# A routing stage and an expert stage joined into one block, with semaphore waits where the engines used to meet

## The chip, the cores and the metric

The kernel runs on one core of one Trainium2 chip. The metric is the time of one execution on the device in microseconds (us). The kernel before took 1334.64 us, the median of three runs (1334.37 to 1336.47).

The engines are named as the profile names them: PE is TensorE (matrix products), DVE is VectorE, ACT is ScalarE, POOL is GpSimd, SP is SyncE (here it only issues DMAs). A q behind a name is that engine's instruction sequencer.

## The reference

The reference is a network on a graph of 3125 nodes with 256 features and 50000 edges: a graph convolution, an attention over slices, a second graph convolution, and a mixture of experts. The change touches the last of the four alone:

```python
logits = xf @ gate_w + gate_b                     # 3125 x 8
probs = softmax(logits)
top2_vals, top2_idx = top_k(probs, 2)
cw = zeros((N, E)).at[arange(N)[:, None], top2_idx].add(top2_vals)
for w1, b1, w2, b2, we in experts:                # 8 experts, 256 -> 512 -> 256
    h = gelu(xf @ w1 + b1)
    acc = acc + we[:, None] * (h @ w2 + b2)
x = x + acc
```

xf is the layer-normed x. Each row goes to two of eight experts, and the kernel computes only those two.

## The kernel before

The rows lie as 25 chunks (NC) of 128 rows (P). After the second graph convolution, two blocks remain. A block gives each engine its own list of instructions; between two blocks all engines meet: each jumps out, waits for the others, and jumps into its next list.

**The routing** is the end of the first of the two blocks. DVE works out each row's two experts and the place of each row in a list of tiles sorted by expert. A tile is 256 rows of one expert ("wide", 2 parts of 128) or 128 rows ("narrow", 1 part); there are 32 tiles (TILES) with 56 parts (HALVES) in all, and every fourth tile is narrow. To turn "row r has place s" into "place s holds row r", DVE writes one-hot matrices: `rhs` (three planes of 56 columns for each of 50 groups) and `oh_lane` (128 columns for each of the 50 groups), lines 1941 to 1948. PE adds 50 products of them up in bank 5 (line 2115), and DVE makes of the sums the integers `row_i` (which row to fetch, line 1954) and `out_i` (where to add the result, line 1958). While DVE works, PE is given 75 products of zeros whose result nobody reads (line 2112, `idle_products(6, 75)`, line 355 in the profile). SP stores the normed rows with their gates in DRAM (`rows_and_gates`) and the residual in `out` at the same time.

**The experts** are the second block. POOL gathers the rows of a tile by an indirect DMA for each part (line 2316, two for a wide tile), three tiles ahead, and SP loads the first weights of a tile's expert, 512 KB (line 2211). The buffer of these weights shares its place with `oh_lane`. For each tile PE transposes the gathered rows (line 2226), DVE copies them to SBUF (line 2289), PE forms the hidden layer in 16 matmuls (line 2243), ACT applies Gelu (line 2274), PE transposes the next tile's rows and then forms the output (line 2258), DVE adds the bias and scales by the gate (lines 2301 and 2304), and POOL adds the rows into `out` by indirect DMAs (line 2336), each tile's after the last one's have landed. The engines are tied by semaphores inside the block. Before the first transposes PE runs 18 more products of zeros (`idle_products(6, 18)`).

`step` is a helper that makes DVE wait until its own last instruction has finished; `e_dv`, `e_pe` and `e_st` count signals of DVE, of PE and of the store of the rows. In DMA rows and orders `agg_in_out` is the memory in which the routing's tables, `row_i` and `out_i` lie.

Of the kernel before, what the change touches and what calls it, by code (L numbers as in the profile page):

```python
# [79 lines left out]
def build(nc, x, src, dst, g0_w, g0_b, w_fx, b_fx, w_x, b_x, w_slice, b_slice, w_q, w_k, w_v,  # L80
# [3 lines left out]
    with ctx:  # L84
# [1666 lines left out]
        def pairs(t3, n):  # L1751
            return t3.unsqueeze(2).to_broadcast([P, 2 * NC, n // 2, 2])

        def twos(t):
            return t.rearrange("p (a d) -> p a d", d=2).unsqueeze(1).to_broadcast([P, 2 * NC, t.shape[1] // 2, 2])
# [3 lines left out]
        with nc.Block() as block:  # L1759
            @block.vector  # L1760
            def _(dve):
# [170 lines left out]
                for k in range(2):  # L1932
# [8 lines left out]
                one_half = rhs[:, :, 0, :].rearrange("p t (a d) -> p t a d", d=2)  # L1941
                step(nc.vector.tensor_tensor(one_half, twos(iota16[:, 0:HALVES]), pairs(half2, HALVES), ALU.is_equal))
                nc.vector.tensor_tensor(rhs[:, :, 1, :].rearrange("p t (a d) -> p t a d", d=2), one_half,
                                        pairs(chunk2, HALVES), ALU.mult)
                nc.vector.tensor_scalar(rhs[:, :, 2, :], rhs[:, :, 0, :], lane[:, 0:1], None, ALU.mult)
                step(nc.vector.tensor_tensor(oh_lane.rearrange("p t (a d) -> p t a d", d=2), twos(iota16[:, :]),
                                             pairs(lane2, P), ALU.is_equal))
                dve.sem_inc(e_dv.sem, 1)

# [4 lines left out]
                nc.vector.tensor_copy(row_i, row_f)  # L1954
# [3 lines left out]
                step(nc.vector.tensor_copy(out_i, out_f))  # L1958
                ch.close(step.done)

            @block.scalar
            def _(act):
# [62 lines left out]
                nc.scalar.activation(prob, lg, ACT.Exp).then_inc(e_ac.sem, 1)  # L2025

            @block.tensor
            def _(pe):
# [91 lines left out]
            @block.sync  # L2120
            def _(sp):
                with nc.allow_non_contiguous_dma(reason="eight gate columns, once"):
                    sp.dma_start(gwt, gate_w.rearrange("(k p) e -> p k e", p=P)).then_inc(e_gl.sem, 16)
                sp.dma_start(gbb, gate_b.partition_broadcast(P)).then_inc(e_gl.sem, 16)
                with sp.If(general(sp)):
                    for s in range(4):
                        general_sum_sp(sp, s)
                    for k in range(3):
                        fetch_seconds(sp, k)
                    fetch_rest(sp)  # L2130
                with sp.Else():
                    def drained(done):
                        s, g = divmod(done - 1, NSB)
                        if s % 2:
                            sp.wait_ge(c_mm.sem, c_mm.at(4 * (s // 2 * NSB + g + 1)))
                        else:
                            sp.wait_ge(a_mm.sem, a_mm.at(5 * (s // 2 * NSB + g + 1)))

                    for s in range(4):
                        for g in range(NSB):  # L2140
                            for k in range(5):
                                matrix_block(sp, s % 2 == 1, s * NSB + g, k, drained)
                            if s == 3 and g < 3:
                                fetch_seconds(sp, g)

                    sp.wait_ge(a_kb.sem, a_kb.at(16 * NSB - 1))
                    fetch_rest(sp)

                sp.wait_ge(e_dv.sem, 3)
                sp.dma_start(zg_dram.rearrange("(c p) f -> p c f", p=P), Z[:, :, :]).then_inc(e_st.sem, 16)  # L2150
                sp.dma_start(out[0:(NC - 1) * P, :].rearrange("(c p) f -> p c f", p=P), XR[:, 0:NC - 1, :]
                             ).then_inc(xr_st.sem, 16)
                sp.dma_start(out[(NC - 1) * P:N, :], XR[0:LAST, NC - 1, :]).then_inc(xr_st.sem, 16)
                sp.wait_ge(e_st.sem, 16)

            @block.gpsimd
            def _(pool):
                with pool.If(general(pool)):
                    for g in range(5):
                        normalise_pool(pool, l_grt, l_gsc, g)  # L2160
                    limit = pool.to_reg(NP - 1)
                    for s in range(4):
                        general_sum_pool(pool, s, limit)
                with pool.Else():
                    for g in range(5):
                        normalise_pool(pool, l_rt, l_sc, g)

                for g in range(5):
                    normalise_pool(pool, l4_rt, l4_sc, g)
                pool.wait_ge(e_lg.sem, BATCHES - 3)  # L2170
                pool.iota(ie, [[1, X]], base=0, channel_multiplier=0, allow_small_or_imprecise_dtypes=True)
                pool.iota(tix, [[1, WIDE]], base=0, channel_multiplier=0, allow_small_or_imprecise_dtypes=True)
                pool.iota(full, [[TP, MOST]], base=TP, channel_multiplier=0, allow_small_or_imprecise_dtypes=True)
                pool.iota(chunk2, [[0, 2], [1, NC], [0, 2]], base=0, channel_multiplier=0,
                          allow_small_or_imprecise_dtypes=True)
                pool.iota(dump, [[P, HALVES]], base=NP, channel_multiplier=1,
                          allow_small_or_imprecise_dtypes=True).then_inc(e_pe.sem, 1)
        e_dv.close(4)
        close_general(4, 2)
        for t, k in ((l_st, 5), (l_rt, 5), (l_sc, 5), (l_z, NC), (l_hi, NC), (a_in, 5), (a_kb, 16 * NSB),   # L2180
                     (a_mm, 2 * NC), (a_lo, 2 * NC), (a_ev, 2 * NC), (x2_in, 2 * NC), (h_in, NC),
                     (c_mm, 8 * NSB), (c_ca, 4 * NSB), (c_cd, 4 * NSB), (p_mm, 2 * NC), (p_out, 2 * NC),
                     *((t, 16 * 4 * NSB) for t in a_ld)):
            t.close(k)

        def is_narrow(n):
            return n % 4 == 3

        def parts(n):
            return 1 if is_narrow(n) else 2  # L2190

        def numbered(n):
            return WIDE + n // 4 if is_narrow(n) else 3 * (n // 4) + n % 4

        def first_half(n):
            return 2 * WIDE + n // 4 if is_narrow(n) else 2 * numbered(n)

        def expert_of(eng, n):
            return eng.value_load(tile_i[0:1, numbered(n):numbered(n) + 1], min_val=0, max_val=X - 1)  # L2199

# [164 lines left out]
```

## Time and profile before

| | before |
|---|---|
| median of three runs | 1334.64 us |
| the profiled execution | 1334.33 us |
| its span, first to last instruction | 1332.6 us |
| granted TensorE clock, mean | 0.969 of full |
| PE busy | 1242.6 us (93%) |
| DVE busy | 570.0 us |
| ACT busy | 473.7 us |
| POOL busy | 198.2 us |

The profiled execution lasted 1.7 us more than its span. The profile counts times from the start of the span. The routing's last part and the start of the experts lie between about 1060 and 1106 us, the 32 tiles behind that up to 1318 us. The clock granted to TensorE is 1.00 (2.4 GHz) or 0.50 (1.2 GHz); a stretch with a value in between holds both.

### The profile page before, as it was taken

How to read it: one execution, taken by the hardware profiler on the slowest of the kernel's cores; microseconds unless marked ns; L12 is line 12 of the kernel's file. 1: busy time of each engine (PE TensorE's matmuls, PEld its weight loads, DVE VectorE, ACT ScalarE, POOL GpSimd, SP SyncE). 2: the span in 40 equal slices, each digit the busy share in tenths (PEclk: the TensorE clock that was granted, in tenths of full speed). 3: DMA queues.
4: the chain of work that ended last, by engine and by line, in shares of the span. 5: the costliest groups of instructions: out<-in, count | busy, mean ns of one | idle time of the engine just before them, and what ended most of it. 6: DMA issues, size and time to landing. Idle time of an engine off the chain costs nothing. (4 is left out here: it accounts for less than half of the span.)

```text
span 1332.6 us, 19869 instructions
## 1 busy us (share of the span) xinstructions
PE 1242.6 (93%) x7442; PEld 844.6 (63%) x7442; DVE 570.0 (43%) x1529; ACT 473.7 (36%) x1142; POOL 198.2 (15%) x201
## 2 busy tenths in 40 slices
PE   3399999989999999999999999999999878999995
PEld 1277777745558544457777544467777547888884
DVE  5878777567764413123333333222222471222221
ACT  5765666357743787830000010001222302222221
POOL 3000000023310000000000000000000005767773
PEclk8599999999999999999999999999999889999998
DMA  5132133400003155575556445587653264666662
GB/s 178 38 124 73 56 121 125 139 28 0 1 0 126 43 157 155 154 157 126 124 128 140 128 148 149 152 188 168 143 120 68 64 198 136 146 142 149 157 156 44
DMA packets 253597, 154.91 MB, mean 116 GB/s; under 512 B 172536, under 2 KB 242375, under 8 KB 253364
## 3 DMA queue, kind: packets, MB, share of 16 engines
q1 hardware_dynamic: 242420, 138.56, 38.0%
q0 software_dynamic: 11072, 14.97, 6.1%
q8 instruction: 64, 1.05, 0.3%
q14 instruction: 41, 0.34, 0.1%
HBM read 78.48 MB, written 35.00 MB: 85 GB/s over the span
## 5 line engine op out<-in xcount | busy, mean ns | idle before, releaser
L974 PE MATMUL bank<-weights,agg_in_out 128*128 128x320 f16 x2000 | 274.8, 299 | 0.0
L988 PE MATMUL bank<-weights 128*128 128x512 f16 x1250 | 270.7, 379 | 1.2 <-issue 1.2
L974 PEld LDWEIGHTS bank<-weights,agg_in_out 128*128 128x128 f16 x2000 | 195.7, 98 | 76.2
L988 PEld LDWEIGHTS bank<-weights 128*128 128x128 f16 x1250 | 122.0, 98 | 149.3 <-DVEq L1786 1.7
L1111 PE MATMUL bank<-weights,agg_in_out 128*128 128x320 f16 x1000 | 163.2, 299 | 0.0
L804 POOL TENSOR_TENSOR shift<-shift,rstd 128x5 f32<-128x5 f32 x15 | 3.6, 243 | 914.6 <-ACT rstd L809 914.6
L519 ACT CAST weights<-bank 128x500 f16<-128x500 f32 x160 | 114.2, 723 | 68.9 <-PE bank L508 68.9
L1111 PEld LDWEIGHTS bank<-weights,agg_in_out 128*128 128x128 f16 x1000 | 91.7, 98 | 26.2
L2258 PE MATMUL bank<-weights 128*128 x448 | 105.5, 384 | 0.5 <-ACT weights L2274 0.2
L2274 ACT ACTIVATE weights<-bank,weights 128x256 f32<-128x256 f32 (+1 forms) x128 | 50.2, 444 | 155.4 <-PE bank L2243 155.4
L2243 PE MATMUL bank<-wk,weights 128*128 128x256 f32 (+1 forms) x512 | 104.2, 357 | 0.9 <-DVE wk L2289 0.9
L1784 DVE SCALAR_TENSOR_TENSOR wk<-bank,inverse_degree,wk 128x256 f32<-128x256 f32 x50 | 24.0, 480 | 181.9 <-ACT wk L1980 181.9
L2336 POOL DMA_INDIRECT out<-weights,agg_in_out x56 | 89.3, 1595 | 61.4 <-DVE weights L2304 34.5
L2243 PEld LDWEIGHTS bank<-wk,weights 128*128 128x128 f32 x512 | 89.5, 193 | 12.0 <-issue 1.2
L2258 PEld LDWEIGHTS bank<-weights 128*128 128x128 f32 x448 | 80.7, 190 | 15.9 <-issue 7.2
L1019 ACT COPY agg_in_out<-bank 128x320 f32<-128x320 f32 x20 | 8.5, 426 | 218.5 <-PE bank L974 218.5
L508 PE MATMUL bank<-wn,wk 128*128 128x125 f16 x640 | 64.8, 227 | 18.2 <-DVE wn L499 17.6
L1027 DVE COPY agg_in_out<-bank 128x320 f32<-128x320 f32 x20 | 9.8, 491 | 161.1 <-PE bank L974 141.0
L498 DVE TENSOR_TENSOR wk<-iota,low_source 128x512 f16<-128x512 f16 x160 | 67.4, 421 | 25.9 <-PE bank L508 25.1
L1980 ACT ACTIVATE wk<-bank,inverse_degree 128x256 f32<-128x256 f32 x50 | 23.6, 474 | 153.2 <-PE bank L988 142.3
L508 PEld LDWEIGHTS bank<-wn,wk 128*128 128x128 f16 x640 | 49.6, 101 | 34.3 <-DVE wn L499 22.8
L2316 POOL DMA_INDIRECT normed<-rows_and_gates,agg_in_out x56 | 59.0, 1054 | 58.5 <-POOLq L1759 41.7
(355 smaller groups left out, 1455.8 us busy)
## 6 DMA issues: line engine op xcount, KB each, us to landing
weights<-counts_source_target SPq DMA_DIRECT2D x50, 800.0 KB, 4.6
counts_source_target<-weights SPq DMA_DIRECT2D x5, 4000.0 KB, 13.9
weights<-in_L_ffn_W SPq DMA_DIRECT2D x32, 512.0 KB, 3.9
weights<-in_L_ffn_W SPq DMA_DIRECT2D x4, 1024.0 KB, 5.5
rows_and_gates<-normed SPq DMA_DIRECT2D x1, 3300.0 KB, 12.0
out<-residual SPq DMA_DIRECT2D x1, 3072.0 KB
residual<-in_x SPq DMA_DIRECT2D x4, 640.0 KB, 7.9
weights<-in_L_ffn_b SPq DMA_DIRECT2D x1, 1024.0 KB, 7.6
```

What stands on the lines that cost most here:

```text
L498: nc.vector.tensor_tensor(couples(ohs[:, u]), ramp(4, P), twins(slo2[:, g, :], P), ALU.is_equal)
L508: last = nc.tensor.matmul(ps[QBANK[u]][:, t * NR:(t + 1) * NR], ohs[:, u, t, :], ohr[:, u, t, 0:NR], start=True, stop=True)
L519: nc.scalar.copy(to, ps[QBANK[q % 4]][:, 0:4 * NR].rearrange("p (t n c) -> p t c n", t=4, c=NC)).then_inc(q_ev.sem, 1)
L974: last = nc.tensor.matmul(bank, source[:, 5 * k + c, part * F + fh * P:part * F + fh * P + P], MB[:, k, c, h * HALF:(h + 1) * HALF], start ...
L988: last = nc.tensor.matmul(ps[j][:, :], MB[:, k, c, j * P:(j + 1) * P], source[:, 5 * k + c, :], start=(k == 0 and c == 0), stop=(k == 4 an ...
L1111: last = nc.tensor.matmul(bank, XH2[:, c, part * F + fh * P:part * F + fh * P + P], ats[b % 2][:, c, h * HALF:(h + 1) * HALF], start=(m == ...
L1784: step(nc.vector.scalar_tensor_tensor(t, ps[n % 5][:, 0:F], inv[:, 1, n:n + 1], wk[:, n % 2, 0:F], ALU.mult, ALU.add))
L2243: last = nc.tensor.matmul(ps[2 + 2 * b + m // 2][:, (m % 2) * w:(m % 2 + 1) * w], w1b[:, b, k, m * P:(m + 1) * P], xT[:, b, k * w:(k + 1) ...
L2258: last = nc.tensor.matmul(ps[6 + b][:, h * F:(h + 1) * F], hT[:, b, k, h * P:(h + 1) * P], w2[:, k, bass.ds(expert, 1), :].rearrange("p a ...
L2274: last = nc.scalar.activation(hT[:, b, m, 0:w], ps[2 + 2 * b + m // 2][:, (m % 2) * w:(m % 2 + 1) * w], ACT.Gelu, bias=b1T[:, bass.ds(expe ...
L2316: pool.indirect_dma_start(out=xg[:, n % 4, h, :], out_offset=None, in_=zg_dram, in_offset=bass.IndirectOffsetOnAxis(ap=row_i[:, t:t + 1], ...
L2336: pool.indirect_dma_start(out=out, in_=yb[:, n % 2, h, :], in_offset=None, out_offset=bass.IndirectOffsetOnAxis(ap=out_i[:, t:t + 1], axis=0),
```

## The change

The second block is gone. Its instructions stand behind those of the routing in the same block, engine by engine, and where the engines met each of them now waits for the semaphores that it needs:

- SP loads the first experts' weights once the 50 products are done (`e_pe` at 3), since they overwrite `oh_lane`.
- POOL starts the gathers once `row_i` is written (`e_dv` at 6, a signal that DVE's copy to `row_i` now gives) and the rows have been stored (`e_st`). DVE works out `out_i` behind that signal.
- ACT waits for `e_dv` at 4, PE and DVE only for the constants loaded long before.
- The one-hots are written in two parts of 25 groups, each followed by a signal, and PE waits for the first signal before group 0 and for the second before group 25.
- At the very end POOL no longer waits for the last results to land; SP still does.

```diff
+                for k in range(2):
+                    at = slice(k * NC, (k + 1) * NC)
+                    one_half = rhs[:, at, 0, :].rearrange("p t (a d) -> p t a d", d=2)
+                    step(nc.vector.tensor_tensor(one_half, twos(iota16[:, 0:HALVES]), pairs(half2[:, at], HALVES),
+                                                 ALU.is_equal))
+                    nc.vector.tensor_tensor(rhs[:, at, 1, :].rearrange("p t (a d) -> p t a d", d=2), one_half,
+                                            pairs(chunk2[:, at], HALVES), ALU.mult)
+                    nc.vector.tensor_scalar(rhs[:, at, 2, :], rhs[:, at, 0, :], lane[:, 0:1], None, ALU.mult)
+                    step(nc.vector.tensor_tensor(oh_lane[:, at].rearrange("p t (a d) -> p t a d", d=2),
+                                                 twos(iota16[:, :]), pairs(lane2[:, at], P), ALU.is_equal))
+                    dve.sem_inc(e_dv.sem, 1)
...
-                nc.vector.tensor_copy(row_i, row_f)
+                nc.vector.tensor_copy(row_i, row_f).then_inc(e_dv.sem, 1)
...
+                dve.wait_ge(e_ld.sem, e_ld.at(16 * (KH + 1 + X)))
...
+                act.wait_ge(e_dv.sem, 4)
+                act.wait_ge(e_ld.sem, e_ld.at(16 * (KH + 1 + X)))
...
                 idle_products(6, 75)
-                pe.wait_ge(e_dv.sem, 4)
                 for t in range(2 * NC):
+                    if t % NC == 0:
+                        pe.wait_ge(e_dv.sem, 4 + t // NC)
                     last = nc.tensor.matmul(ps[5][:, 0:3 * HALVES], oh_lane[:, t, :],
...
                 last.then_inc(e_pe.sem, 1)
+                pe.wait_ge(e_ld.sem, e_ld.at(16 * (KH + 1 + X)))
...
+                idle_products(6, 18)
+                turn(0)
...
-                sp.wait_ge(e_st.sem, 16)
+                sp.wait_ge(e_pe.sem, 3)
+                for n in range(TILES):
+                    expert = expert_of(sp, n)
...
-        with nc.Block() as block:
...
+                pool.wait_ge(e_st.sem, 16)
+                pool.wait_ge(e_dv.sem, 6)
+                gather(pool, 0)
+                for n in range(1, 3):
+                    gather(pool, n)
...
-                for b in range(2):
-                    pool.wait_ge(y_st[b].sem, scattered(TILES - 2 + b))
```

The order of DVE's instructions before, from the one-hots of `rhs` to the copy of the first tile; `weights` is the memory of `oh_lane`, `bank` is PSUM:

```order
L1942 TENSOR_TENSOR agg_in_out<-iota,agg_in_out 128x50x56 [waits dve_step]
L1943 TENSOR_TENSOR agg_in_out<-agg_in_out 128x50x56 [waits dve_step]
L1945 TENSOR_SCALAR agg_in_out<-agg_in_out,lane 128x50x56
L1946 TENSOR_TENSOR weights<-iota,agg_in_out 128x6400
L1951 COPY agg_in_out<-bank 128x56 [waits dve_step,routing_sums]
...
L1958 CAST agg_in_out<-agg_in_out 128x56 [waits dve_step]
L1759 UNCONDITIONAL_BRANCH [waits dve_step]
L2280 UNCONDITIONAL_BRANCH [waits barrier_Pool_Activation_PE_DVE_SP_release]
L2289 COPY wk<-bank 128x512 [waits tile_transposed]
```

And the same place of DVE now:

```order
L1970 TENSOR_TENSOR agg_in_out<-iota,agg_in_out 128x25x56 [waits dve_step]
L1972 TENSOR_TENSOR agg_in_out<-agg_in_out 128x25x56 [waits dve_step]
L1974 TENSOR_SCALAR agg_in_out<-agg_in_out,lane 128x25x56
L1975 TENSOR_TENSOR weights<-iota,agg_in_out 128x3200
L1970 TENSOR_TENSOR agg_in_out<-iota,agg_in_out 128x25x56 [waits dve_step]
L1972 TENSOR_TENSOR agg_in_out<-agg_in_out 128x25x56 [waits dve_step]
L1974 TENSOR_SCALAR agg_in_out<-agg_in_out,lane 128x25x56
L1975 TENSOR_TENSOR weights<-iota,agg_in_out 128x3200
L1980 COPY agg_in_out<-bank 128x56 [waits dve_step,routing_sums]
...
L1987 CAST agg_in_out<-agg_in_out 128x56 [waits dve_step]
L1997 COPY wk<-bank 128x512 [waits tile_transposed,expert_constants,dve_step]
```

Four instructions have become eight of half the size, and the two branches of the meeting are gone.

POOL before, from its last table of the routing to the first result that it adds into `out`:

```order
L2176 IOTA agg_in_out 128x56
L1759 UNCONDITIONAL_BRANCH
L2311 UNCONDITIONAL_BRANCH [waits barrier_Pool_Activation_PE_DVE_SP_gather]
L2316 DMA normed<-rows_and_gates,agg_in_out 128x264 x7
L2336 DMA out<-weights,agg_in_out 3125x256 [waits residual_stored,expert_out_ready]
```

And POOL now:

```order
L2304 IOTA agg_in_out 128x56
L1772 DMA normed<-rows_and_gates,agg_in_out 128x264 [waits routing_ready,rows_and_gates_stored]
L1772 DMA normed<-rows_and_gates,agg_in_out 128x264 x6
L2324 DMA out<-weights,agg_in_out 3125x256 [waits residual_stored,expert_out_ready]
L2324 DMA out<-weights,agg_in_out 3125x256
```

The same seven gathers stand ahead of the first result; the first of them carries the waits (`routing_ready` is `e_dv`).

PE now, from the 75 products of zeros to the first tile's hidden layer (before, the 50 products were one run with one wait, followed by the two branches of the meeting):

```order
L355 MATMUL bank<-zeros,ident 128x512 x75
L2190 MATMUL bank<-agg_in_out,weights 128x168 [waits routing_ready]
L2190 MATMUL bank<-agg_in_out,weights 128x168 x24
L2190 MATMUL bank<-agg_in_out,weights 128x168 [waits routing_ready]
L2190 MATMUL bank<-agg_in_out,weights 128x168 x24
L355 MATMUL bank<-zeros,ident 128x512 [waits expert_constants]
L355 MATMUL bank<-zeros,ident 128x512 x17
L2202 MATMUL bank<-ident,normed 128x128 [waits tile_gathered0]
```

The 25 products of the first part can run before the second part is written, but not before the 75 products of zeros that stand ahead of them.

## Rows read from the trace of the kernel before

**Rows 1.** The chain of waits; start, length, what the time went to

```profile
1099.46 5.18 DMA normed<-rows_and_gates,agg_in_out
...
1106.21 5.38 PE bank L2243 x16
...
1115.78 3.45 PE bank L2243 x16
```

**Rows 2.** Timeline: start, length, engine, line, what [idle before <-releaser]

```profile
1079.73 10.31 PE L355 MATMUL bank<-zeros,ident 128*128 128x512 f16 x47
...
1083.78 1.62 DVE L1942 TENSOR_TENSOR agg_in_out<-iota,agg_in_out 128x2800 f16<-128x2800 f16 x1
1085.43 1.62 DVE L1943 TENSOR_TENSOR agg_in_out<-agg_in_out 128x2800 f16<-128x2800 f16 x1
1086.96 0.94 DVE L1945 TENSOR_SCALAR agg_in_out<-agg_in_out,lane 128x2800 f16<-128x2800 f16 x1
1087.82 3.48 DVE L1946 TENSOR_TENSOR weights<-iota,agg_in_out 128x6400 f16<-128x6400 f16 x1
...
1091.42 3.80 PE L2115 MATMUL bank<-agg_in_out,weights 128*128 128x168 f16 x50 [1.39 <-DVEq L1948]
...
1095.76 0.19 DVE L1954 CAST agg_in_out<-agg_in_out 128x56 int32<-128x56 f32 x1
...
1096.61 0.19 DVE L1958 CAST agg_in_out<-agg_in_out 128x56 int32<-128x56 f32 x1
...
1097.35 4.05 PE L355 MATMUL bank<-zeros,ident 128*128 128x512 f16 x18 [2.13 <-PEq L1759]
1098.10 1.05 POOL L2316 DMA_INDIRECT normed<-rows_and_gates,agg_in_out  x1 [41.72 <-POOLq L1759]
1098.27 47.72 SPq L2211 DMA_DIRECT2D weights<-in_L_ffn_W  x8
...
1104.68 0.66 PE L2226 MATMUL bank<-ident,normed 128*128 128x128 f32 x4 [3.29 <-DMA normed<-rows_and_gates,agg_in_out]
1104.72 1.01 POOL L2316 DMA_INDIRECT normed<-rows_and_gates,agg_in_out  x1 [0.30 <-issue]
1105.38 0.69 DVE L2289 COPY wk<-bank 128x512 f32<-128x512 f32 x1 [8.57 <-PE bank L2226]
...
1109.78 1.28 ACT L2274 ACT_TABLE_LOAD   x1 [46.84 <-PE bank L2243]
```

**Rows 3.** Timeline: DVE around its signal at line 1877

```profile
1069.62 0.37 DVE L1876 TENSOR_TENSOR agg_in_out<-agg_in_out,valid 128x200 f32<-128x200 f32 x1
...
1070.13 0.37 DVE L1878 TENSOR_TENSOR normed<-agg_in_out 128x200 f32<-128x200 f32 x1
```

**Rows 4.** Timeline: POOL released by DVE, at tile 1

```profile
1124.20 0.67 DVE L2304 TENSOR_SCALAR weights<-weights,normed 128x256 f32<-128x256 f32 x2
...
1125.69 1.63 POOL L2336 DMA_INDIRECT out<-weights,agg_in_out  x1 [1.17 <-DVE weights L2304]
```

**Rows 5.** Lines 2199 (SP), 2211 and 2316 alone, 1090 to 1140, 1120 and 1108

```profile
L2199 SPq TENSOR_LOAD <-agg_in_out x8: 263/274/464, 1097.3 to 1138.6; - x8
...
DMA to landing us min/median/max: 3.5/3.8/5.9
...
DMA to landing us min/median/max: 3.1/3.9/5.2
```

**Rows 6.** Stretches: length, busy (x count) PE PEld DVE ACT POOL, PEclk, DMA, GB/s

```profile
1072.00:1076.00 4.00, 4.00 (x11) 1.46 (x10) 3.69 (x21) 0.00 (x0) 0.00 (x0) 0.52 1.05 357
1076.00:1080.00 4.00, 4.00 (x21) 1.82 (x19) 3.65 (x22) 0.00 (x0) 0.00 (x0) 1.00 1.09 341
...
1106.00:1107.00 1.00, 0.79 (x3) 0.70 (x4) 0.07 (x1) 0.00 (x0) 0.97 (x1) 0.77 0.46 101
...
1110.00:1111.00 1.00, 1.00 (x7) 0.87 (x5) 0.00 (x0) 1.00 (x1) 0.00 (x0) 1.00 0.00 0
```

**Rows 7.** The page's part on DMA issues: count, KB each, us to landing

```profile
rows_and_gates<-normed SPq DMA_DIRECT2D x1, 3300.0 KB, 12.0
```

More of the change, by code:

```diff
@@ L2025, in _ @@
                 nc.scalar.activation(prob, lg, ACT.Exp).then_inc(e_ac.sem, 1)
+                act.wait_ge(e_dv.sem, 4)
+                act.wait_ge(e_ld.sem, e_ld.at(16 * (KH + 1 + X)))
+                for n in range(TILES):
+                    b = n % 2
+                    w = parts(n) * P
+                    expert = expert_of(act, n)
+                    if n >= 2:
+                        act.wait_ge(y_mm.sem, n - 1)
+                    for m in range(KH):
+                        if m % 2 == 0:
+                            act.wait_ge(h_mm.sem, 2 * n + m // 2 + 1)
+                        last = nc.scalar.activation(hT[:, b, m, 0:w],
+                                                    ps[2 + 2 * b + m // 2][:, (m % 2) * w:(m % 2 + 1) * w], ACT.Gelu,
+                                                    bias=b1T[:, bass.ds(expert, 1), m:m + 1].rearrange("p a k -> p (a k)"))
+                        if m % 2:
+                            last.then_inc(h_ac.sem, 1)
             @block.tensor
@@ L2118, in _ @@
                 last.then_inc(e_pe.sem, 1)
[L2120 to L2153, printed above, removed]
-                sp.wait_ge(e_st.sem, 16)
@@ L2156, in _ @@
[L2156 to L2199, printed above, removed]
-        def scattered(n):
-            return 16 * sum(parts(j) for j in range(n % 2, n + 1, 2))
@@ L2311, in _ @@
+                        sp.wait_ge(h_mm.sem, 2 * (n - 1))
+                    sp.dma_start(w1b[:, n % 2], e_w1[bass.ds(expert, 1)].rearrange("a (k p) n -> p (a k) n", p=P)
+                                 ).then_inc(w_ld[n % 2].sem, 16)
+                for b in range(2):
+                    sp.wait_ge(y_st[b].sem, scattered(TILES - 2 + b))
             @block.gpsimd
             def _(pool):
-                def gather(n):
-                    for h in range(parts(n)):
-                        t = first_half(n) + h
-                        pool.indirect_dma_start(
-                            out=xg[:, n % 4, h, :], out_offset=None, in_=zg_dram,
-                            in_offset=bass.IndirectOffsetOnAxis(ap=row_i[:, t:t + 1], axis=0),
-                            bounds_check=NP - 1, oob_is_err=False).then_inc(x_ld[n % 4].sem, 16)
@@ L2321, in _ @@
-                for n in range(3):
-                    gather(n)
+                with pool.If(general(pool)):
+                    for g in range(5):
+                        normalise_pool(pool, l_grt, l_gsc, g)
+                    limit = pool.to_reg(NP - 1)
+                    for s in range(4):
+                        general_sum_pool(pool, s, limit)
+                with pool.Else():
+                    for g in range(5):
+                        normalise_pool(pool, l_rt, l_sc, g)
+                for g in range(5):
+                    normalise_pool(pool, l4_rt, l4_sc, g)
```

147 lines of the change are left out of this document (84 added, 63 removed).

## The prediction

> **What bounds the kernel now.** I read the chain of waits first, since it says which engine each moment of the end rests on. From 1106.21 us on it is PE almost without a break: 16 products of a hidden layer, 3.45 us when the clock is full, then transposes and output, tile after tile. Ahead of that stands one long transfer, 5.18 us, the second gather of tile 0 [rows 1]. So nothing in the 32 tiles waits for the routing, and the change can win only what it brings the first product of the experts forward; this start moves everything behind it.
>
> Next the timeline, to see what that start hangs on. The reader is to follow one string of it: DVE writes one-hots from 1083.78 to 1091.30, PE's 50 products run from 1091.42 to 1095.22, `row_i` is written at 1095.95 (1095.76 + 0.19), DVE ends at 1096.80, POOL's first gather begins at 1098.10, the gathers land, PE transposes at 1104.68, DVE copies, and at 1106.21 the hidden layer starts [rows 1, 2]. Every link waits for the one ahead. Last the stretches, for the clock: the 16 products at 1106.21 took 5.38 us and not 3.45, since the granted clock fell to 1.2 GHz within 1106 to 1107 and was back at 1110 [rows 1, 6].
>
> **The one-hots in two parts.** The four instructions take 1.62, 1.62, 0.94 and 3.48 us for 2800, 2800, 2800 and 6400 columns [rows 2]. The first and the last are of one kind: (3.48 − 1.62) / 3600 columns is 0.517 ns a column, which leaves 0.17 us that doesn't shrink. Halves thus cost 0.90, 0.90 and 1.83 us. The third is of another kind; I give it half its time above the same 0.17, 0.55 us. Its start and that of the fourth overlap the one ahead by 0.09 and 0.08 us, and the first's end is awaited, 0.03 us, so one part costs 0.90 + 0.03 + 0.90 − 0.09 + 0.55 − 0.08 + 1.83 = 4.04 us. Between the parts stands a signal by itself. The row for that is line 1877: DVE ended at 1069.99 and began again at 1070.13, 0.14 us [rows 3]. Part 0 is ready at 1083.78 + 4.04 = 1087.82, part 1 at 1087.82 + 0.14 + 4.04 = 1092.00, 0.70 us later than all of it before.
>
> PE can't use part 0 at 1087.82: the 75 products of zeros end only at 1079.73 + 10.31 = 1090.04 [rows 2]. From there the first 25 products take 25 × 0.076 = 1.90 us (3.80 / 50), until 1091.94. Part 1 releases PE 0.12 us after it is ready, as before (1091.30 to 1091.42), at 1092.12, and the last 25 products end at 1094.02 instead of 1095.22. The gain is 1.20 us. Its bounds: 1.9 us if halving cost DVE nothing, 0.5 us if it cost double the 0.70.
>
> **The meeting.** DVE needs the same 0.73 us from PE's end to `row_i`: 1094.75. How long POOL then takes is not in this place of the trace, as it came out of a branch. The nearest row is tile 1, where POOL was released by DVE for an indirect DMA as well: DVE ended at 1124.87, POOL's DMA began at 1125.69, 0.82 us [rows 4]. The first gather then starts at 1095.57, 2.53 us earlier than 1098.10; of this 1.33 is the meeting together with the four instructions for `out_i`, which now run behind POOL's signal and beside its wake-up. The bounds of the wake-up are 0.30 us, POOL's pause between two gathers [rows 2], and 1.30 us, from DVE's end at 1096.80 to 1098.10 with the meeting in it. With the first split as taken they put the gain at 3.05 or 2.05 us. I keep 0.82, since it is the same release and the same kind of DMA.
>
> What else is moved: SP's loads of weights. SP took 0.97 us from its read of the tile table at 1097.3 to the issue at 1098.27 [rows 2, 5]. It is now released by PE's end, so the issue comes at about 1094.02 + 0.05 + 0.97 = 1095.04, 3.23 us earlier. The store of the rows had no wait on SP's path worth counting: it is issued behind DVE's line 1877 at about 1070 and took 12.0 us to land [rows 3, 7], so it is over by about 1083, and the residual's store runs on as before. ACT's load of the Gelu table still stands behind its first wait (1.28 us, [rows 2]), ahead of the output products, in the same place of the chain: nothing. The other engines' waits for constants are for transfers long landed: nothing. At the end POOL's missing wait gives nothing, as SP still waits for the same transfers.
>
> **The landing.** Tile 0's second gather took 5.18 us, where the shortest of the seven took 3.1 and the median is 3.9 [rows 1, 5]. It shared the DMA engines with two loads of 512 KB, the slower of which took 5.9 us [rows 5], so until about 1104.2. Now the loads are issued 3.23 us earlier and the gathers 2.53, so 0.70 us more of the loads is over when the second gather starts. Bounds: −2.1 us if the loads were out of the way (3.1 instead of 5.18), +0.7 if the head start went against the gather, the loads' data being served first. I take −0.3, somewhat under half of the head start, since the loads still lie across most of the gather.
>
> Here the trace shows the two kinds in flight together and a slow gather, not how they share. The Trainium skill, "DMA: Bandwidth & Descriptors", section "Queues, rings and completion order", says that each DMA engine takes packets in turn from the queues that have work. By it a head start of the loads can only help a gather, up to 0.7 us, and the sum would come out 0.4 us lower; no run here shows the turns.
>
> **The clock.** The 18 products of zeros follow the 50 directly and end at about 1094.1 + 4.05 = 1098.15. The gather lands at 1095.57 + 1.36 + 5.18 − 0.30 = 1101.81, so PE pauses for 3.7 us, where it paused 3.28 (1101.40 to 1104.68) [rows 2]. The low stretch cost 5.38 − 3.45 = 1.93 us [rows 1]. I leave it at that: nought. Bounds: −1.9 us if the clock doesn't fall, +0.7 if it falls before the transposes. They then take 0.66 us longer, and the hidden layer loses half of the low time in it. The longest low time with PE busy that the rows show is 3.85 us: PE was busy through 1072 to 1076, and a mean of 0.52 there puts the rise at 1075.85 [rows 6]. That is 0.66 + 1.93 − 1.93.
>
> **Sum.** Gather start −2.53, landing −0.30, clock 0: −2.83 us. On the profiled execution 1334.33 − 2.83 = 1331.50. It lies 0.31 us under the median of the runs, so the forecast for the median is 1331.8 us. A difference of 0.2%, 2.67 us here, is about what a measurement can tell from no change; the forecast stands just beyond it, at 1331.97.
>
> **Rivals.**
>
> 1. *The split gives little.* If DVE's halves cost 1.4 us more than the whole, the gain falls to 0.5 on that part, and the sum to 1.33 + 0.5 + 0.3 = 2.1: 1332.5 us. For it speaks that the third instruction's fixed part is a guess; against it, that the fixed part of the others comes from two rows.
> 2. *The landing is what holds, and takes the place of the meeting.* The gather starts early but lands no earlier than the loads let it: 5.18 + 0.7 us. Then 2.53 − 0.7 = 1.8 us are won: 1332.8 us. For it: a gather's worst landing was here. Against it: the loads move forward by more than the gathers.
> 3. *The clock doesn't fall before or in tile 0.* −1.9 us more: 1329.9 us. Against it: PE's pause grows, and during a shorter one it fell.
> 4. *The clock falls before the transposes.* +0.7 us: 1332.5 us. The pause is 0.4 us longer, which speaks for it; the transposes and the hidden layer still follow each other as before. The Trainium skill, "TensorE: Matmul & The Clock Gate", Part 1, ties the clock to how busy PE has been of late; by that rule this time is the one to expect if the pause decides. That the clock fell soon after the pause agrees, at 1106 to 1107 [rows 6].
> 5. *Slower.* The clock falls in the longer pause and stays at 1.2 GHz into the first tiles. Each us of low running costs 0.5. Over the 1.93 us paid now, it takes 2.83 + 1.93 = 4.8 us of loss, 9.5 us of low running, to eat the gain, and 15 us to be 0.2% slower: 1337.3 us. Against it: with PE running without a pause the clock rose at 1075.85 and, in tile 0, by 1110 [rows 6]. For it only that rises are seen at two places.
> 6. *The change doesn't do what it says*: POOL's first gather waits for something late, such as the store of the rows. That landed by about 1083, so there is nothing for it.
>
> **How the numbers follow.** The forecast has 0.52, with its own range of 1331.0 to 1332.4; rivals 1, 2 and 4 have 0.30 together, rival 3 has 0.12, rival 5 has 0.05, and rival 6 has 0.01. Faster by over 0.2% are rival 3 and some four fifths of the forecast's share: 0.54. Slower by over 0.2% is rival 5: 0.05. Within 0.2% is the rest, 0.41. The range goes from 1329.8, where the clock's rival stands, to 1333.5, half the gain lost; it leaves out rival 5 and the outer ends of the others.
>
> **What would show it.** In the profile after: the 50 products as two runs, the first beginning at about 1090.0 and the second ending near 1094.0; POOL's first gather at about 1095.6 and 0.8 us after DVE's copy to `row_i`; SP's first load at about 1095.0, ahead of it; the transposes of tile 0 near 1101.8; the first hidden layer near 1103.4, again with some 5.4 us for its 16 products; and from there the tiles at the old pace, with the last product near 1315.3. I am wrong if the second run of products waits beyond 1092.5, if the gather takes well over or under 5 us to land, or if the granted clock's low stretch changes its length or is gone.

## The result, and the profile after

The changed kernel took 1331.81 us, median of seven runs (1330.52 to 1332.78), against 1335.22 us for the kernel before in seven runs of its own. The ratio is 0.9972, with a 95% interval of 0.9962 to 0.9981: 0.28% faster. The forecast was 1331.8 us. The profiled execution took 1330.82 us with a span of 1329.0, 3.5 us less than the profiled one of before.

The timeline of the changed kernel from DVE's first one-hot on (start, length, engine, line, what, [idle before <-releaser]) answers to [rows 2]:

```profile
1084.40 0.89 DVE L1970 TENSOR_TENSOR agg_in_out<-iota,agg_in_out 128x1400 f16<-128x1400 f16 x1
...
1088.59 0.89 DVE L1970 TENSOR_TENSOR agg_in_out<-iota,agg_in_out 128x1400 f16<-128x1400 f16 x1
...
1090.42 1.98 PE L2190 MATMUL bank<-agg_in_out,weights 128*128 128x168 f16 x25
1090.83 1.81 DVE L1975 TENSOR_TENSOR weights<-iota,agg_in_out 128x3200 f16<-128x3200 f16 x1
...
1092.75 1.99 PE L2190 MATMUL bank<-agg_in_out,weights 128*128 128x168 f16 x25 [0.35 <-DVEq L1977]
...
1094.57 4.05 PE L355 MATMUL bank<-zeros,ident 128*128 128x512 f16 x18
...
1095.27 0.19 DVE L1983 CAST agg_in_out<-agg_in_out 128x56 int32<-128x56 f32 x1
...
1095.71 21.76 SPq L2278 DMA_DIRECT2D weights<-in_L_ffn_W  x4
...
1096.40 1.05 POOL L1772 DMA_INDIRECT normed<-rows_and_gates,agg_in_out  x1 [39.41 <-DVE agg_in_out L1983]
1097.75 1.01 POOL L1772 DMA_INDIRECT normed<-rows_and_gates,agg_in_out  x1 [0.30 <-issue]
...
1102.15 0.66 PE L2202 MATMUL bank<-ident,normed 128*128 128x128 f32 x4 [3.53 <-DMA normed<-rows_and_gates,agg_in_out]
...
1103.79 5.29 PE L2219 MATMUL bank<-wk,weights 128*128 128x256 f32 x16 [0.98 <-DVE wk L1997]
1107.47 1.28 ACT L2095 ACT_TABLE_LOAD   x1 [43.92 <-PE bank L2219]
...
1109.75 3.72 PE L2234 MATMUL bank<-weights 128*128 x16 [0.24 <-ACT weights L2095]
```

The one-hots begin at 1084.40, where they began at 1083.78 before: the unchanged program ahead of them took 0.62 us longer in this execution. Read from each profile's own first one-hot, the links of the string compare as follows (us):

| link | before | after | gain | forecast |
|---|---|---|---|---|
| first one-hot to the end of the 50 products | 11.44 | 10.33 | 1.11 | 1.20 |
| to POOL's first gather | 2.88 | 1.67 | 1.21 | 1.33 |
| second gather to the transposes (1.36 between the gathers) | 5.22 | 4.40 | 0.82 | 0.30 |
| transposes to the first hidden product | 1.53 | 1.64 | −0.11 | 0 |
| to the first output product | 5.85 | 5.96 | −0.11 | 0 |
| to the last product | 206.06 | 206.34 | −0.28 | 0 |
| to the end of the span | 14.45 | 12.94 | 1.51 | 0 |

They add up to 4.15 us; less the 0.62 ahead of them that is the 3.5 of the profiles. Most of the forecast's string is there. What wasn't in it stands in the last row: nobody had touched the last tile, and yet the end came 1.5 us closer to the last product. Two rows of the sequencers show where, one of the kernel before and one of the kernel after (line, engine's sequencer, instruction, count, shortest/median/longest in ns, first and last start):

```profile
L2204 POOLq DRAIN  x1: 6312/6312/6312, 1326.0 to 1326.0; - x1
```

```profile
L1785 POOLq DRAIN  x1: 8092/8092/8092, 1320.7 to 1320.7; - x1
```

At the end of a block each engine drains. POOL's drain before started at 1326.0, once the last results had landed, and took 6.31 us, to 1332.3; behind it only the engines' closing signals stand, up to the span's end at 1332.6. Now its row starts at 1320.7, 0.2 us ahead of the last scatter's own (1320.93 to 1322.48), and ends at 1328.8, 6.3 us behind that instruction. So the landing of the last results, which POOL waited for, now lies beside the 6.3 us and not ahead of them.

The clock's low stretch came again. The columns are length, busy (x count) of PE, PEld, DVE, ACT, POOL, the granted clock, DMA share, GB/s:

```profile
1102.00:1103.00 1.00, 0.66 (x4) 0.42 (x4) 0.05 (x1) 0.00 (x0) 0.69 (x1) 1.00 0.51 135
1103.00:1104.00 1.00, 0.21 (x1) 0.24 (x2) 0.64 (x1) 0.00 (x0) 1.00 (x1) 0.80 0.51 131
1104.00:1105.00 1.00, 1.00 (x3) 0.82 (x4) 0.00 (x0) 0.00 (x0) 0.70 (x2) 0.50 0.24 63
...
1107.00:1108.00 1.00, 1.00 (x6) 0.90 (x5) 0.00 (x0) 0.53 (x1) 0.00 (x0) 0.99 0.16 34
```

The first hidden product ran 2.42 us earlier by the clock on the wall, and the clock fell 3 us earlier with it, so that the 16 products took 5.29 us and not the 3.7 of a full clock.

### The profile page after: what moved, and what is told of

The parts are those of the page before. It is cut to its first block, busy times and chain, and to the rows that moved or that the text cites. A ratio compares the mean times of both kernels' runs of the same rounds, so it can differ in the third digit from the quotient of the medians.

```text
span 1329.0 us, 19862 instructions
## 1 busy us (share of the span) xinstructions
PE 1242.5 (93%) x7442; PEld 844.6 (64%) x7442; DVE 570.7 (43%) x1533; ACT 473.8 (36%) x1142; POOL 198.3 (15%) x201
## 4 chain that ended last, share of the span: by engine, by line
PE 63%; DVE 4%; issue 1%; DMA 1%; ACT 0%; POOLq 0%; POOL 0%; DVEq 0%; ACTq 0%
PE bank L974 20%; PE bank L988 20%; PE bank L2234 7%; PE bank L2219 7%; PE bank L1009 2%; PE bank L1615 2%; PE bank L2202 1%; PE bank L1731 1%; PE bank L1723 0%; PE bank L355 0%; DVE bnbuf L788 0%; DVE weights L1855 0%; DVE tb L1820 0%; DMA normed<-rows_and_gates,agg_in_out 0%; DMA out<-weights,agg_in_out 0%
## 5 line engine op out<-in xcount | busy, mean ns | idle before, releaser
L2095 ACT ACTIVATE weights<-bank,weights 128x256 f32<-128x256 f32 (+1 forms) x128 | 50.2, 444 | 155.7 <-PE bank L2219 155.5
```

The lines of the kernel that those rows point to most:

```text
L2095: last = nc.scalar.activation(hT[:, b, m, 0:w], ps[2 + 2 * b + m // 2][:, (m % 2) * w:(m % 2 + 1) * w], ACT.Gelu, bias=b1T[:, bass.ds(expe ...
```

## The experiments

Two theories. **The first**: three things ahead of tile 0 share the gain, the products' end, the start of the gather and its landing, and the rest is the drain at the end; each moves the end by its own size. **Its rival**: the start of the gathers is worth little, since something else sets when tile 0 can be computed at full speed (the loads beside the gather, the clock), and the gain is the split's and the end's. Each kernel ran with runs of the kernel before on the same chip; the ratios below are to those. The median of before was 1335.22 us beside the first four kernels below, 1335.37 beside the next four and 1336.3 beside the last four, so that times of different groups compare to about 1 us only.

**POOL's last wait back in the changed kernel, and out of the kernel before.**

The first, on the changed kernel, is

```diff
+                for b in range(2):
+                    pool.wait_ge(y_st[b].sem, scattered(TILES - 2 + b))
```

and the second is the kernel before without the same two lines.

> The changed kernel, with POOL's wait for the last results put back ahead of its closing drain. Theory (the drain behind POOL's last DMA takes 6.3 us and starts later if POOL waits first): 1.4 us slower than the changed kernel, 1333.2 us, and the drain starts about 1.4 us after POOL's last DMA instruction ends. Rival (the end of the kernel hangs on SP's wait, POOL's own is worth nothing): 1331.8 us, no difference.

> The kernel before, with nothing changed but POOL's last wait taken away. Theory of the drain: 1.4 us faster than before, 1333.8 us against 1335.2, with the routing and the start of the experts as they were. Rival: 1335.2 us.

Measured: 1333.2 us, ratio 0.9986 (0.9977 to 0.9995), with the wait back; 1333.73 us, ratio 0.9988 (0.9979 to 0.9997), without it in the kernel before. Both are where the theory of the drain has them (1333.2 and 1333.8), and the second interval leaves out 1. The drains, of the first and the second kernel:

```profile
L1785 POOLq DRAIN  x1: 6302/6302/6302, 1325.5 to 1325.5; - x1
```

```profile
L2204 POOLq DRAIN  x1: 8088/8088/8088, 1325.0 to 1325.0; - x1
```

With the wait the drain takes 6.3 us and follows the landing; without it, it takes 8.1 and starts with the last scatter. From the end of the last product to the end of the span the two kernels with the wait need 14.4 and 14.5 us in their profiles, and all twelve without it 12.9 to 13.1. This is shown: some 1.4 to 1.5 of the 3.4 us come from two lines at the very end.

**The one-hots whole again.**

```diff
...
-                for k in range(2):
-                    at = slice(k * NC, (k + 1) * NC)
+                for k in range(1):
+                    at = slice(0, 2 * NC)
...
```

> The changed kernel with the one-hots in one part again. If the two parts are worth what the profile shows between DVE's first one-hot and the end of PE's 50 products (11.44 us before, 10.35 after): 1.1 us slower than the changed kernel, 1332.9 us. Rival (the gather lands when the weights' loads let it, so an earlier row_i is given back in the landing): under 0.4 us slower, the second gather's landing shorter by what row_i is later.

Measured: 1333.14 us, ratio 0.9985 (0.9976 to 0.9994), some 1.3 us over the changed kernel where 1.1 was expected; the two intervals overlap a little. From the first one-hot the products end at 11.44 us, the first gather starts at 13.10 instead of 12.00, and the transposes at 19.28 instead of 17.75. Nothing was given back in the landing (4.82 us from the second gather to the transposes).

**The meeting kept, with the split and without POOL's last wait.**

It is the kernel before with the one-hots in two parts as in the change, and

```diff
-                for b in range(2):
-                    pool.wait_ge(y_st[b].sem, scattered(TILES - 2 + b))
```

> The changed kernel with the two blocks apart, so with the meeting, but with the one-hots in two parts and without POOL's last wait. Theory: the meeting and the four instructions for out_i come back (1.2 us from the end of the products to the first gather), and with them the gather's longer landing (up to 0.8 us, since the loads no longer have a head start): 1.2 to 2.0 us slower than the changed kernel, 1333.0 to 1333.8 us. Rival (only the tail and the split count): 1331.8 us.

Measured: 1330.68 us, ratio 0.9967 (0.9955 to 0.9979). It is no slower than the changed kernel; if anything, it is 1 us faster. It was expected at 1333.0 to 1333.8 by the first theory, which falls here. The timeline:

```profile
1092.90 1.99 PE L2119 MATMUL bank<-agg_in_out,weights 128*128 128x168 f16 x25 [0.28 <-DVEq L1951]
...
1097.02 5.73 PE L355 MATMUL bank<-zeros,ident 128*128 128x512 f16 x18 [2.13 <-PEq L1759]
1097.77 1.05 POOL L2320 DMA_INDIRECT normed<-rows_and_gates,agg_in_out  x1 [40.62 <-POOLq L1759]
...
1099.12 1.01 POOL L2320 DMA_INDIRECT normed<-rows_and_gates,agg_in_out  x1 [0.30 <-issue]
...
1103.99 0.66 PE L2230 MATMUL bank<-ident,normed 128*128 128x128 f32 x4 [1.24 <-DMA normed<-rows_and_gates,agg_in_out]
...
1105.52 3.69 PE L2247 MATMUL bank<-wk,weights 128*128 128x256 f32 x16 [0.87 <-DVE wk L2293]
```

Its first one-hot began at 1084.56. The meeting costs what the profile promised: first gather at 13.21 us from there (changed kernel 12.00), transposes at 19.44 (17.75), first hidden product at 20.96 (19.39). But the 16 hidden products take 3.69 us, not 5.29, and the first output product starts at 25.33, where the changed kernel has 25.35. The granted clock tells what took the gain:

```profile
1097.00:1098.00 1.00, 0.98 (x3) 0.42 (x4) 0.00 (x0) 0.00 (x0) 0.23 (x1) 0.54 0.00 0
...
1102.00:1103.00 1.00, 0.75 (x4) 0.14 (x2) 0.00 (x0) 0.00 (x0) 0.76 (x1) 1.00 0.91 324
...
1106.00:1107.00 1.00, 1.00 (x6) 0.87 (x6) 0.00 (x0) 0.00 (x0) 0.71 (x1) 1.00 0.55 127
```

Here the low stretch lay on the products of zeros, which nobody waits for. They ran longer, 5.73 us, filled the pause before the transposes but for 1.24 us, and the clock stayed at full speed for the real work. In the changed kernel the zeros run at full speed, end early, PE pauses for 3.5 us, and the low stretch falls on the hidden layer.

What brought it onto the zeros is not shown. The 2.1 us that PE idles in the meeting are not enough: the kernel before idles the same 2.13 us and then runs the zeros in 4.05 [rows 2], and so does the kernel before without POOL's last wait, whose clock fell only behind them:

```profile
1098.98 4.04 PE L355 MATMUL bank<-zeros,ident 128*128 128x512 f16 x18 [2.13 <-PEq L1759]
...
1106.10 1.11 PE L2226 MATMUL bank<-ident,normed 128*128 128x128 f32 x4 [3.07 <-DMA normed<-rows_and_gates,agg_in_out]
...
1108.09 5.66 PE L2243 MATMUL bank<-wk,weights 128*128 128x256 f32 x16 [0.88 <-DVE wk L2289]
```

Four of the kernels, all without POOL's last wait, make a table of the split and the meeting (us):

| | one-hots whole | one-hots in two parts |
|---|---|---|
| blocks apart | 1333.73 (before_no_tail_wait) | 1330.68 (meeting_kept) |
| blocks joined | 1333.14 (whole_onehots) | 1331.81 (the changed kernel) |

The parts don't add up. The split brings the end of the 50 products 1.1 us forward in either row of the table, and moves the time by 3.05 us with the meeting and by 1.33 without it. In the profiles of the upper row the first output product comes 3.5 us earlier, and 2.4 of them are the transposes and the hidden layer at a fuller clock (1.11 and 5.66 us against 0.66 and 3.69). Joining gives 0.6 us with whole one-hots and loses 1.1 with the split; the intervals tell neither from nothing.

**More zeros in the changed kernel.** If the clock has eaten the gain, which is theory A in the expectations from here on, filling the pause should return it.

```diff
-                idle_products(6, 18)
+                idle_products(6, 34)
                 turn(0)
```

> The changed kernel with 34 products of zeros ahead of tile 0's transposes instead of 18. Theory A (what the joined blocks bring forward is eaten by the granted clock: PE pauses 3.7 us before the transposes, the clock falls, and the first eight hidden products take 3.4 us instead of 1.7): the products fill the pause, the first eight take 1.7 us, 1.3 to 1.7 us faster than the changed kernel, 1330.1 to 1330.5 us. Rival B (the clock falls at its own time whatever PE does, and the meeting is worth nothing since the gather's landing sets the start): the transposes start no earlier and the time is the changed kernel's, 1331.8 us, or up to 0.3 more if the zeros delay them.

Measured: 1330.14 us, ratio 0.9970 (0.9957 to 0.9982).

```profile
1094.61 7.50 PE L355 MATMUL bank<-zeros,ident 128*128 128x512 f16 x34
...
1102.41 0.66 PE L2202 MATMUL bank<-ident,normed 128*128 128x128 f32 x4 [0.30 <-issue]
...
1104.05 3.69 PE L2219 MATMUL bank<-wk,weights 128*128 128x256 f32 x16 [0.98 <-DVE wk L1997]
...
1106.14 1.28 ACT L2095 ACT_TABLE_LOAD   x1 [42.57 <-issue]
```

The hidden layer takes 3.69 us and the first output product starts 23.98 us from the first one-hot, 1.37 earlier than in the changed kernel. The median went down by 1.7 us, the upper end of what theory A had (1.3 to 1.7); since the ratio's interval overlaps the changed kernel's, the rows carry more than the time does. One more number agrees: the clock granted over a whole execution was 0.970 or 0.971 of full in each of these six runs, and 0.968 or 0.969 in each of the changed kernel's seven.

**ACT's table load taken off the string**, alone and with 34 products.

```diff
                 nc.scalar.activation(prob, lg, ACT.Exp).then_inc(e_ac.sem, 1)
+                nc.scalar.activation(yb[:, 0, 0, 0:1], ones[:, 0:1], ACT.Gelu)
```

> The changed kernel with the early table load alone. The chain of the changed kernel shows PE waiting 0.2 us for ACT before the first output products: 0.2 us faster, 1331.6 us, not to be told from no change. Rival (the chain's whole ACT piece, 1.3 us, goes): 1330.5 us.

> The same with ACT's Gelu table loaded right after the Exp, by an activation of one column. Theory A: with the clock full, ACT's 1.28 us of table load behind the first eight products is what the first output products wait for; taking it off the chain gives some 0.5 us more, 1329.7 us. Rival (the table load lies beside PE's second eight products, as the chain of the kernel before had it): the same as with 34 products alone.

Measured: 1331.62 us alone, ratio 0.9973 (0.9964 to 0.9982), and 1329.5 us with 34 products, ratio 0.9967 (0.9955 to 0.9979). Alone it can't be told from no change. With the clock full, the time from the first hidden to the first output product went from 4.37 us (34 products) to 3.96, so 0.4 us are real on the string, but they are within what these runs can tell.

**The signal for the rows given late.**

```diff
-                nc.vector.tensor_copy(row_i, row_f).then_inc(e_dv.sem, 1)
+                nc.vector.tensor_copy(row_i, row_f)
...
                 step(nc.vector.tensor_copy(out_i, out_f))
+                dve.sem_inc(e_dv.sem, 1)
```

> The changed kernel with DVE's signal to POOL only after out_i, so four instructions (0.66 us) and a signal by itself (0.1 us) later. If each step of the chain to the first gather counts in full: 0.8 us slower, 1332.6 us. Under theory A it depends on where the granted clock's low stretch then lies: the gather, the transposes and the first hidden product are each 0.8 us later, and the end anything from 0 to 0.8.

Measured: 1331.72 us, ratio 0.9977 (0.9968 to 0.9986): no loss that can be told, where 0.8 us was expected if each step counts in full. The rows say more than the time. The first one-hot was at 1084.13:

```profile
1097.03 1.05 POOL L1772 DMA_INDIRECT normed<-rows_and_gates,agg_in_out  x1 [40.33 <-DVEq L1988]
...
1098.39 1.01 POOL L1772 DMA_INDIRECT normed<-rows_and_gates,agg_in_out  x1 [0.30 <-issue]
...
1101.50 1.11 PE L2203 MATMUL bank<-ident,normed 128*128 128x128 f32 x4 [3.16 <-DMA normed<-rows_and_gates,agg_in_out]
```

The second gather was issued 0.9 us later from the one-hot (14.26 against 13.35), and the transposes started not later but 0.4 earlier (17.37 against 17.75). It landed in 3.1 us instead of 4.4. So the landing isn't a fixed span behind the issue.

**The loads moved against the gathers.** Earlier (with `oh_lane` in a place of its own, so that they need not wait for the products), together with the rows, and behind tile 0's gather.

The early loads:

```diff
-        oh_lane = BIG[:, 10304:10304 + 2 * NC * P // 2].bitcast(F16).rearrange("p (t n) -> p t n", n=P)
+        oh_lane = BIG[:, 12352:12352 + 2 * NC * P // 2].bitcast(F16).rearrange("p (t n) -> p t n", n=P)
...
-                sp.wait_ge(e_pe.sem, 3)
+                sp.wait_ge(e_dv.sem, 4)
```

The other two, of which the first line is in loads_with_rows and the second in loads_behind:

```diff
                 sp.wait_ge(e_pe.sem, 3)
+                sp.wait_ge(e_dv.sem, 6)
...
+                sp.wait_ge(x_ld[0].sem, 32)
```

> The changed kernel with oh_lane moved to a place that the first experts' weights don't use, so that SP loads them at DVE's first signal (7 us before the gathers) and not after the products. Theory (tile 0's second gather takes 4.3 to 5.2 us to land since the two loads of 512 KB are in flight beside it): it lands 3.1 us after its issue, transposes and first hidden product come 1.2 to 1.8 us earlier; the end 0 to 1.8 us earlier, by where the granted clock's low stretch lies: 1330 to 1331.8 us. Rival (a first gather takes this long whatever is beside it, as POOL is generating the next ones): landing and time unchanged.

> The changed kernel with SP's first loads held until row_i is written, 0.7 us later, so that loads and gathers start together. Theory: the second gather lands 5.0 us or more after its issue, as before the change: transposes 0.3 to 0.7 us later, the time 1331.8 to 1332.5 us. Rival (the landing doesn't depend on the loads): unchanged in both.

> The changed kernel with SP's first loads held until tile 0's rows have landed: a look at the gather with no load beside it. Theory: the second gather lands 3 us after its issue. The hidden layer then waits for its weights, 3.6 us or more after the landing, so the whole is some 1.5 us slower than the changed kernel. Rival: 4.4 us or more as in the changed kernel.

Measured: 1330.35 us, ratio 0.9950 (0.9937 to 0.9964), for the early loads; 1333.2 us, ratio 0.9975 (0.9966 to 0.9985), with the rows, 0.7 us above the 1331.8 to 1332.5 expected; 1333.26 us in the one run behind the gather. From the issue of the second gather to the transposes:

| SP's first load, from the first gather | second gather to transposes |
|---|---|
| 6.2 us ahead (early_loads) | 2.88 |
| 1.6 us ahead (rows_with_outs) | 3.11 |
| 0.7 us ahead (changed kernel) | 4.40 |
| 0.1 us behind (loads_with_rows) | 5.04 |
| 0.2 us behind (kernel before) | 5.22 |
| 5.6 us behind (loads_behind) | 2.85 |

The two ends in rows, first of the loads behind, then of the loads with the rows:

```profile
1097.41 1.01 POOL L1772 DMA_INDIRECT normed<-rows_and_gates,agg_in_out  x1 [0.30 <-issue]
...
1100.26 0.93 PE L2202 MATMUL bank<-ident,normed 128*128 128x128 f32 x4 [1.99 <-DMA normed<-rows_and_gates,agg_in_out]
```

```profile
1097.63 1.01 POOL L1772 DMA_INDIRECT normed<-rows_and_gates,agg_in_out  x1 [0.30 <-issue]
...
1102.67 0.66 PE L2202 MATMUL bank<-ident,normed 128*128 128x128 f32 x4 [4.17 <-DMA normed<-rows_and_gates,agg_in_out]
```

A gather with no load beside it lands in 2.9 us; the loads add up to 2.4. POOL generated the next gathers beside all of them, so the rival, that this alone makes tile 0's gather slow, falls by the two ends of the table. Its middle is not told so finely. Five other kernels had the changed kernel's head start of 0.7 us, and their values are 4.62 (34 products, where PE came to the transposes only then), 4.77, 4.82, 4.95 and 5.21 us; the two others with the meeting (0.2 us behind) had 4.87 and 5.01. So the 5.04 with the rows lies inside what a head start of 0.7 us gives too. With the rows, the tiles also took 2 us longer in the profile, of which two waits of PE of 0.7 us each are 1.4; I found no cause, and the other profiles scatter there too (206.0 to 208.6 us from the first output product to the last).

The early loads alone show again what the clock does. In the profiled execution, which took 1333.24 us, the hidden layer started at 17.92 us from the one-hot, 1.5 us before the changed kernel's, and then took 6.45 us. The five runs of this kernel fall apart by the clock granted over the whole execution: 1328.59 and 1328.83 us at 0.971, and 1330.35 to 1333.24 us at 0.968 or 0.969. That suggests that the same program meets the low stretch in one execution and not in another; only the execution of 1333.24 us has a profile.

**The three together**: early loads, 29 products of zeros (the pause is shorter), the early table.

> The same with 29 products of zeros, which fill PE's pause up to the earlier landing, and ACT's Gelu table loaded early. If the three are what stood ahead of tile 0 (loads beside the gather, the clock, the table): 1.2 to 1.8 us faster than 34 products with the early table, 1327.7 to 1328.3 us. Rival (landing unchanged): 1329.5 us.

Measured: 1328.05 us (1327.23 to 1328.86), ratio 0.9936 (0.9922 to 0.9949). It beats both kernels: 0.64% under the kernel before, more than twice the change's own gain. The clock over the whole execution was 0.971 in all five runs.

```profile
1091.63 16.52 SPq L2279 DMA_DIRECT2D weights<-in_L_ffn_W  x3
...
1099.25 1.01 POOL L1772 DMA_INDIRECT normed<-rows_and_gates,agg_in_out  x1 [0.30 <-issue]
...
1102.33 0.60 PE L2203 MATMUL bank<-ident,normed 128*128 128x128 f32 x4
...
1103.91 3.69 PE L2220 MATMUL bank<-wk,weights 128*128 128x256 f32 x16 [0.98 <-DVE wk L1997]
```

With the first one-hot at 1085.90, the hidden layer starts at 18.01 us and the first output product at 21.97, against 19.39 and 25.35 in the changed kernel.

## Why the prediction was right, and where it wasn't

- **The split** (1.20 forecast) measured 1.11. The second run of products was released at 1092.75, 8.35 us from the first one-hot against 8.34 forecast. The part that was a guess, the third instruction, took 0.59 us instead of 0.55. The kernel with the one-hots whole lost it again. The upper bound of 1.9 us was wrong by its own working: PE is busy with the first 25 products until 1091.94, so that even with halves that cost nothing the last product would end at 1093.84, a gain of 1.4.
- **The meeting** (1.33) measured 1.21. POOL's wake-up was 0.94 us (1095.46 to 1096.40) instead of the 0.82 of [rows 4]; the bounds held it.
- **The landing** (−0.3) measured −0.8 in this pair of profiles. That the loads beside it make the gather slow was right: 2.9 us alone, 5.0 with them. What the head start is worth, one pair can't say: over all profiles the mean is 4.8 us with the head start of 0.7 us (six kernels, 4.40 to 5.21) and 5.0 with the loads 0.2 us behind (three, 4.87 to 5.22). That is 0.2 us, near the forecast's 0.3 and smaller than the scatter; the 0.8 is in part luck. The rule of the Trainium skill that the DMA engines take packets in turn ("DMA: Bandwidth & Descriptors", "Queues, rings and completion order") agrees in sign with the two means; no run here shows the turns.
- **The clock** (0) came out at 0: the hidden layer took 5.29 us against 5.38, and the low stretch lay on the same products in both. The price beside it was misread. The 3.45 us for a hidden layer at a full clock is a row of the chain, which leaves out the start of the first product; tile 0's takes 3.69, so the low stretch cost 1.7 us and not 1.93. And that it stays was an assumption, not a reading. Against the kernel with the meeting kept, what joining brings forward up to the hidden layer, 1.6 us, the low stretch takes back; with 34 products of zeros it is gone; and rival 4, the clock falling before the transposes, did come in four other profiles (before_no_tail_wait, tail_wait_back, gelu_table_early, rows_with_outs), where they took 1.11 or 1.12 us instead of 0.66, a loss of 0.45 there and not the 0.66 reckoned.
- **ACT's table load** ("nothing") cost 0.24 us: PE waited for it before the first output products, [0.24 <-ACT weights L2095].
- **POOL's last wait** is the step that failed: "At the end POOL's missing wait gives nothing, as SP still waits for the same transfers." It gave about 1.4 us. That SP still waits is true; what I didn't look at is what POOL does behind its wait. The row of its drain was in the trace of before, 6.31 us that nothing covered, ending with the span.

So the sum of 2.83 us came near the measured 3.41 with two errors in it, and that is luck for a good part: what the end gave unforeseen was set off by links that gave less. That the median came out at the forecast's 1331.8 to the hundredth is luck as well, since the kernel before had meanwhile measured 1335.22 and not the 1334.64 that the forecast starts from. In the profiles the end gave 1.5 us and the landing 0.5 more than forecast; the other links gave 0.7 less, and the program ahead of the change took 0.62 longer. Of the signs of being wrong, the second run of products waited until 1092.75, beyond the 1092.5 named, but only by the 0.62 us that the program ahead took longer; the gather's 4.40 us is under the 5 named, which the scatter above covers. In the medians the account is: the end gives 1.4 to 1.5 us, the split 1.3 in the joined kernel, and joining the blocks at this place adds nothing that these runs can tell (1331.81 with, 1330.68 without). The upper end of the range, called half the gain lost, would by that be 1333.2 and not 1333.5; nothing hangs on it.

What stays open: why the low stretch came 2.2 us behind the products in meeting_kept, and 8.4 to 11.3 us behind them in the two kernels with the same 2.13 us of idle PE. meeting_kept rests on one profile and on six runs of 1330.23 to 1332.5 us; I didn't try the meeting with a clock kept full through it, and each kernel has one profile only.

## What to carry to other kernels

Price a removed wait by what stands behind it on its own engine, sequencer instructions included: a wait that others make as well can still hold up a drain of 6 us. When work is brought forward ahead of a stretch of PE work, ask what PE does in the pause that grows: time won in front of it can be taken back whole by the granted clock, and products of zeros must be counted anew. The split won 3.05 us with the meeting in place and 1.33 without it, so try two steps each with and without the other. And when two kinds of DMA become free at one moment, look at which of them the next stage needs first; here issuing 1 MB of weights 5.5 us earlier brought the transposes forward by 1.5 us, and taking out the meeting brought the first gather forward by 1.2.

## What the runs showed of the hardware that I had not expected

- POOL's drain ended 6.3 us after its last indirect DMA instruction when nothing was waited for in between, and took 6.3 us from its own start when it began after that DMA had landed: 6.31, 6.30 us in two kernels with the wait, 8.09 in those without it, counted from 0.2 us ahead of the last scatter's start.
- The granted clock fell in meeting_kept within 2.2 us of the end of the second products and cost nothing, and in the changed kernel some 1.5 us after the gather landed and cost 1.6 us. The Trainium skill's "TensorE: Matmul & The Clock Gate", Part 1, ties the clock to how busy PE has been of late. Both falls came behind an idle stretch of PE, which agrees; but in the kernel before the same 2.13 us of idle were followed by 4.05 us at full clock, so the last idle stretch alone doesn't tell when it falls.
- An indirect gather of 128 rows landed in 2.9 us alone and in 4.9 to 5.2 us (four kernels) with two loads of 512 KB issued within 0.2 us of it.
